# A fused decoder kernel on one core: the same items of work in another written-out order

## The reference

```
x = ln(x + L0_attn(x))     # 16 heads, xpos rotation, causal
x = ln(x + L0_xattn(x, ctx))
x = ln(x + L0_ffn(x))      # quantised linear, depthwise conv, silu, quantised linear
x = ln(x + L1_attn(x))     # attention over the 16 heads inside each token
x = ln(x + L1_xattn(x, ctx, mask))
x = ln(x + L1_ffn(x))      # 16 experts, top 2, capacity
x = ln(x + L2_attn(x))     # 16 heads, rotation, causal
x = ln(x + L2_xattn(ctx, x, ctx, mask))
x = ln(x + L2_ffn(x))      # gated, then two 512x512 layers
x = ln(x + L3_attn(x))     # one head, distance bias
x = ln(x + L3_xattn(x, ctx, ctx))
x = ln(x + L3_ffn(x))      # 8 experts, gated
```

## Time and profile before

| | |
|---|---|
| median of three runs | 1619.02 us |
| the profiled execution | 1613.98 us |
| its span in the trace | 1612.3 us |
| TensorE busy | 1322.0 us, 8762 matmuls |
| VectorE busy | 1094.0 us |
| ScalarE busy | 742.5 us |
| GpSimd busy | 363.0 us |
| granted TensorE clock, mean | 0.913 of 2.4 GHz |

### The profile page before, as it was taken

One profiled execution on the slowest core, in us unless ns is written; L12 is line 12 of the kernel. 1 busy time (PEld: TensorE's weight loads), 2 busy tenths in 40 slices (PEclk: granted clock), 3 DMA queues, 4 the chain that ended last, 5 costly groups with the idle time before them and its releaser, 6 DMA issues.

```text
span 1612.3 us, 24326 instructions
## 1 busy us (share of the span) xinstructions
PE 1322.0 (82%) x8762; PEld 612.3 (38%) x8762; DVE 1094.0 (68%) x2373; ACT 742.5 (46%) x1040; POOL 363.0 (23%) x470
## 2 busy tenths in 40 slices
PE   4586997876557688687789997999999999978986
PEld 2233332332222343343235544434444444434453
DVE  4674777889999778988877675763335522358665
ACT  1046565654424324214367642565745543534742
POOL 2224253105243404333631120121311100110000
PEclk8688899997767789899799999999999999999989
DMA  6521043200020210321232223130313220033111
GB/s 157 149 61 45 19 93 62 42 2 1 1 39 16 54 41 25 79 64 31 52 79 49 69 60 77 60 84 19 88 25 55 66 81 28 1 76 67 32 46 44
DMA packets 50354, 86.26 MB, mean 53 GB/s; under 512 B 13750, under 2 KB 42230, under 8 KB 45942
## 3 DMA queue, kind: packets, MB, share of 16 engines
q1 hardware_dynamic: 50238, 84.71, 22.5%
HBM read 66.95 MB, written 15.60 MB: 51 GB/s over the span
## 4 chain that ended last, share of the span: by engine, by line
PE 50%; DVE 26%; issue 6%; DMA 5%; ACT 5%; SPq 4%; POOL 3%; ACTq 0%; DVEq 0%; POOLq 0%
PE ps L910 6%; PE ps L1064 6%; PE ps L836 6%; DVE MX L1279 6%; PE ps L1030 4%; PE ps L1037 4%; PE ps L1031 4%; PE ps L843 3%; DMA KH<-scratch 2%; PE ps L871 2%; PE ps L792 2%; DVE pack L1420 2%; DVE HEADS L1431 2%; SPq L2055 2%; DVE HEADS L1422 2%
## 5 line engine op out<-in xcount | busy, mean ns | idle before, releaser
L1279 DVE TENSOR_REDUCE MX<-ps 128x3 f32<-128x462 f32 (+5 forms) x704 | 412.0, 627 | 136.5 <-PE ps L843 113.1
L1710 ACT ACTIVATE WORK<-ps 128x1024 f32<-128x1024 f32 (+1 forms) x352 | 318.9, 945 | 143.7 <-PE ps L871 112.5
L836 PE MATMUL ps<-KH,QH 48*128 48x154 bf16 (+5 forms) x1536 | 139.1, 267 | 107.4 <-DVE MX L1279 61.6
L910 PE MATMUL ps<-WORK,VA 128*18 128x512 f32 (+3 forms) x1536 | 163.8, 514 | 9.8 <-POOL WORK L1951 9.0
L1804 ACT ACTIVATE SIDE<-ps 128x512 f32<-128x512 f32 x96 | 56.9, 597 | 234.8 <-PE ps L1031 234.7
L1951 POOL TENSOR_SCALAR_AFFINE_SELECT WORK<-WORK 128x256 f32<-128x256 f32 (+1 forms) x192 | 93.3, 494 | 297.1 <-ACT WORK L1710 296.7
L1965 POOL TENSOR_TENSOR HEADS<-HEADS 128x512 f32<-128x512 f32 x64 | 106.0, 1690 | 239.5 <-DVE HEADS L1432 132.1
L836 PEld LDWEIGHTS ps<-KH,QH 48*128 48x128 bf16 (+1 forms) x1536 | 60.3, 96 | 262.1 <-DVE MX L1279 150.0
L1037 PE MATMUL ps<-SIDE 128*128 128x128 f32 x768 | 111.6, 295 | 23.2 <-DVE SIDE L1530 20.0
L1530 DVE TENSOR_TENSOR SIDE<-SIDE,ps 128x512 f32<-128x512 f32 x96 | 65.5, 686 | 91.0 <-ACT SIDE L1804 90.7
L871 PE MATMUL ps<-QH,KH 54*128 54x512 bf16 (+3 forms) x768 | 116.7, 345 | 10.7 <-ACT WORK L1710 7.0
(11 more groups left out here) (285 smaller groups left out, 2149.8 us busy)
## 6 DMA issues: line engine op xcount, KB each, us to landing
SIDE<-in_experts SPq DMA_DIRECT2D x96, 192.0 KB, 2.4
scratch<-HQ SPq DMA_DIRECT2D x48, 192.0 KB, 2.9
QH<-scratch SPq DMA_DIRECT2D x48, 192.0 KB
SIDE<-in_wide SPq DMA_DIRECT2D x8, 1024.0 KB, 6.0
QH<-scratch SPq DMA_DIRECT2D x48, 128.0 KB
scratch<-HK SPq DMA_DIRECT2D x16, 192.0 KB, 3.0
QH<-scratch SPq DMA_DIRECT2D x48, 64.0 KB
KH<-scratch SPq DMA_DIRECT2D x16, 192.0 KB
```

Of the source, the lines that this page charges most:

```text
L836: mms[b] = pe.matmul(banks[b][:, c * pitch:c * pitch + width], qr[b][:, h, t * 128:t * 128 + 128], kr[b][:, h, 0:width], start=(c == 0), s ...
L910: mm = pe.matmul(ps[32 * j:32 * j + 2 * NV, UB, q0:S], lhsT.rearrange("p a c -> p (a c)"), PB[:, (PAIR_BASE[F] + where[pi]) % NSLOT, b, at ...
L1279: dve.tensor_reduce(MX[:, 32 * b + i0:32 * b + i0 + cnt], src, AX.X, ALU.max, negate=True).then_inc(freed, 1)
L1710: act.activation(PB[:, N % NSLOT, :, lo:hi], wide_banks("pair", F, n)[:, :, lo:hi], ACT.Exp).then_inc(sem("exp_done"), 1)
```

## The change

Only the text `STEPS` changes. It has the same words in the same numbers (1986 words, 2338 items with each `max` counted as two), and `FRONT_ORDER`, `SIDE_ORDER` and `TAIL_ORDER` are as before, so each kind still passes through its stages, batches and numbers in the same sequence; what moves is how the kinds are interleaved. The waits are the same by their rule, with counts that follow the new list. The functions that do the work are not touched. Below is the start of both texts and the lines in which the prediction's steps can be found.

```diff
@@ -255,76 +255,79 @@
 STEPS = """
-project*5 pieces send base project*5 max*2 pieces max*2 project max project max*5 project max*2 project max*2 send max
-project max*4 pieces max*3 split project max turn max project max pair*2 max*2 pair max pair*2 max value max pair value
-max value max project max pair*2 max pair max send value max pair*2 max value pair max value max pair value pair max
-value copy pair max pair max value max pair*2 max pair split pair out value pair max pair turn value max pair value max
-pair value max value pair max value pair max pair value max copy pair*2 max value max project pair max value max pair
-out pair max pair*2 max value mix pair project value*2 pieces value rest pair max value pair max pair max value pair max
-pair*2 max send wo max copy value max value square pair max pair*2 max mean value split value x max pair project*2 turn
...
-value*2 pair max pair copy wo max value send max square pair mean max value x max pair split project value pair*2 turn
...
-project mix pair max value pair max pair project split wo copy pieces out value send turn max value max square pair mean
...
-log ew x qkv top ew gu project*2 ew rank gu project dn ew project pieces hv dn gu hs dn ew hm send hv gu*2 qkv dn ew dn
...
-project out max pair*2 max project*2 mix max pair*2 max value max pair pieces max pair*2 max value max wo copy send pair
-max square value max value max split mean value x copy turn out*2 project*3 mix project pair*2 max wo pair*2 max square
...
-hid2 wo x square hid2 mean x wo project*2 f3 square mean turn s3 project s3 project pair fk3 pieces pt3*2 value pt3*2 x
...
+project*5 pieces base send max*2 project max*2 project max*2 project max project max project max pieces max project
+max project max*2 project max*3 project max*2 rest send max*2 project max pieces max split project max turn pair max
+pair max project pair max pair*3 max value pair max*2 pair value max send pair*2 value max value pair max value max*2
+pair value max pair max value*2 pair copy max pair max value pair max project max*2 pair*2 value max pair project
+value max pair max pair split max pair value pair max turn max out pair max value pair value*2 pair*2 max value pair
+max pair*2 copy max project max*2 value*2 max pieces out pair max*2 pair max pair value mix max pair*2 value max pair
+value*2 max pair wo pair*2 max value pair max value pair max square copy value max pair value pair*2 max mean send max
...
+pair out max pair value pair x pair max value split value max value project value project value turn max pair project
...
+pair*2 mix value out value send wo turn square max pair*2 max pair value copy max mean out max x mix max*2 wo square
...
+ew project*2 hs rank pieces send dn gu hv ew max gu ew max dn max hm qkv ew gu max dn gu ew max dn max gu max ew dn
...
+project value max out value max copy square out max mean max mix max split wo project pieces x send turn square max
...
+square hid2 mean x wo project*2 f3 turn pair square s3 project s3 project fk3 pair value pt3*3 pieces pt3 pair mean
...
 """.split()
```

More of the change, by code:

```diff
@@ L273 @@
[L273 to L282, removed]
@@ new lines @@
+pair*2 max value max mean pair x project max value pair*2 q0x value pair*2 project max q0t project max split h0*2 copy
+silu0 value project out value silu0 pieces turn value silu0*2 send copy h0t*2 pair out h0b pair h0b h0t mix wo h0t
+pair h0b square max mean max h0b x pair*2 max wo max*2 q0x pair max value pair value*2 copy pair q0t pair max out max
+h0*2 value square max pair value mean value silu0 max*2 split silu0 x silu0*2 copy h0t turn h0t pair h0b pair h0t pair
+h0b qkv h0t pair h0b pair out qkv mix value hs hv value wo value pair copy pair square hs pair mean qkv hm pair x hv
@@ new lines @@
+h0b hs out pair qkv wo hm q0x square value q0t hs hv value hm value h0 copy hv out h0 silu0*3 mix hm silu0 mean wo h0t
+square ht x mean wo square h0t mean x h0b*2 x h0t qkv project*2 h0t h0b qkv project h0b hs project pieces send wo hv
+q0x square hs max*2 q0t max hm qkv hv max h0 max h0 max*2 silu0 qkv silu0 max silu0 max silu0 max*2 split h0t*2 turn
+h0b pair*2 hs pair h0t value pair hm mean pair h0b value h0t h0b pair h0b pair value copy hv hs hm wo pair*2 value x
+pair value*2 out copy hv square out hm mix mean wo x ht qkv wo square*2 mean x mean x log ew project*2 qkv top gu hs
@@ new lines @@
+dn max*2 project max hm project ew*2 max gu*2 project max ew dn max qkv max ew project max dn max ew gu pieces max gu
+max dn max gu max send dn max split ew gu dn hv max ew gu dn turn dn max pair acc max pair wo square max pair*2 max
+mean pair max pair x qkv project*3 hs project*2 pieces value*2 pair hm pair value pair max pair*3 hv max value*2 send
+pair value pair hs pair*2 max*2 value pair max value copy split hm pair value turn pair*2 value pair value pair max
+pair out pair max value hv max value max value*2 max value hm copy pair*3 value max pair out value max pair ht pair
@@ new lines @@
+gu copy dn ew*2 out*2 gu dn max split gu ew dn max ew gu dn max gu dn ew max gu dn max ew*2 gu dn max ew gu dn max ew
+gu turn max dn gu ew dn max gu mix pair max wo max dn square max value dn max pair*2 acc max pair wo square mean pair
+max mean max x*2 pair wide pair max value project max pair project max pair project w3 project max g2*2 value max g2
+max g2 project max pieces send hid2 split turn copy hid2 max value pair max pair hid2 max value pair max pair value
+max pair out copy max pair*2 value max pair*2 value pair max pair value max pair value pair max pair value*2 wide max
@@ new lines @@
+pair out value max pair mix pair value max copy wo max pair*2 value*2 pair max out pair value max square pair*2 value
+max pair mean max pair hid2 max value*4 max copy hid2 out max hid2 max split x hid2 mix turn hid2 wo pair*2 square wo
+pair*2 mean pair value wide x pair value pair project pair g2 project*2 g2 project g2 pieces square send g2 pair mean
+hid2*3 pair max value max pair value pair*2 max pair value*2 max value pair value copy max pair value pair max pair*2
+out pair max value x pair*2 wide max value*2 max pair*2 hid2 max value*4 copy max hid2 split out hid2 mix hid2 wo
@@ new lines @@
+hid2 out hid2 mix hid2 max pair wo pair max square hid2 max pair value max wo max pair mean max pair value x pair max
+value wide pair max copy square g2*2 value max g2*2 wide pair value max pair hid2 split hid2*3 turn value mean copy
+out hid2*2 out hid2 x mix hid2 wo pair*2 wo f3 square mean square s3*2 fk3 value pt3*2 pair pt3*2 mean pair x pair x
+wo f3 square pair mean s3 x s3 value pair value pt3*2 fk3 pt3*2 copy project*2 wo log pair project ew top square pair
+project value ew*2 pair value mean gu*2 x pieces value out copy send dn*2 gu max project max dn ew max ew gu max
```

74 lines of the change are left out of this document (31 added, 43 removed).

## The result

The changed kernel takes 1647.57 us (median; 1639.21 to 1650.70) against 1619.17 us for the kernel before: a ratio of 1.0169, 95% interval 1.0129 to 1.0209. The profiled execution took 1646.09 us, its span is 1644.4 us and its mean granted clock 0.902 (before: 1613.98, 1612.3 and 0.913).

The account below looks back on a forecast made before the run. TensorE was taken to bound the kernel (work plus 290 us of idle), VectorE being fuller from 250 to 800 us. Terms -12 + 4 + 34 - 3 - 4 = +19 us gave 1638 us; own case 1625 to 1652, range 1602 to 1668.

Parts of the forecast that it names:

- parts 3 and 4: Waits from short cover behind `turn` and `send`: 30.9 us outside 250 to 800 us, 29.3 inside; taken +34 us.
- Part 1: `rest` comes 154 places earlier, into L0a.0's maxima where ScalarE idles, so TensorE's 11.97 us wait goes; taken -12 us.
- Part 2: L0a.1's projections move from the free wait for L0a.0's keys to among the first maxima; taken +4 us.
- Part 3: `turn` to first `pair`: work between falls short of 3.8 us; missing cover over all fronts grows from 6.4 to 34.7 us.
- Part 3's and 4's weighting by stretch: Waits outside 250 to 800 us counted whole, inside half since VectorE is fuller there: 45.6 us, times 0.75.
- Part 4: Operands and weights behind `send` get less cover: missing 14.1 us more outside 250 to 800 us, 17.8 inside.
- Parts 5 and 6: ScalarE's table reloads fall from 80 to 72, taken -3 us; TensorE's waits ahead of the experts' `dn` shrink, taken -4.
- A: Rival: faster, short cover hides as VectorE sets the pace and waits fall on existing idle; -15 us, 1604 us; chance 0.18.
- B: Rival: much slower, all 60 us show as a waiting TensorE starves VectorE of its three banks; 1664 us; chance 0.22.
- C: Rival: no change in time, local gains and losses cancel; 1619 us; chance 0.07.
- D: Rival: `rest` stalls as long in its new place, its ScalarE work held up by late weights; 1650 us; chance 0.06.

Follow-up runs that it names:

- the two kernels with one edit each: Kernel before with only `rest` moved early: 1623.43 us, ratio 1.0015; kernel before with only L0a.1's and L0a.2's projections moved late: 1616.90 us, ratio 0.9978.
- operands late: Kernel before with projections, pieces and send of L0x.2, L1x.1, L1x.3, L2x.1 and L3x.0 moved down: 1666.22 us, ratio 1.0276.
- both early edits: Kernel before with `rest` moved early and L0a.1's and L0a.2's projections put among L0a.0's maxima: 1611.98 us, ratio 0.9957.
- three bare turns: Kernel before with the first pair directly behind `turn` for L0a.3, L0x.1 and L0x.3: 1635.93 us, ratio 1.0078.
- middle alone: Kernel before with only items 245 to 697 in the new order: 1652.04 us, ratio 1.0194.
- eight bare turns: Kernel before with the first pair of eight fronts pulled up behind `turn` or the last pair of the front before: 1654.15 us, ratio 1.0207.
- turns covered: Changed kernel with each front's first pairs held behind `turn` until about 4 us of other work, then let go together: 1665.22 us, ratio 1.0267 to before.
- covered evenly: Changed kernel with each front's pairs and what follows delayed behind `turn` by a queue, let go one by one: 1687.44 us, ratio 1.0401 to before.
- tail alone: Kernel before with only items 698 to the end in the new order: 1616.48 us, ratio 0.9989.

## Why the prediction was right

- **Sign, range and the sum of idle.** The sum was +19 us of idle; the page has +17.5. That agreement is luck, as the places show: the forecast had two thirds of the idle of parts 3 and 4 outside 250 to 800 us, and at equal work TensorE's idle grows by 16.5 us between the cuts, falls by 1.5 us behind them (168.4 to 166.9) and grows by about 2.5 us ahead of them. Too little was charged in the middle, and in the tail the gains were put too low. The median stands 10 us above the forecast and the sum had no term for the clock, which is worth 14.6 us of busy time in the pair of profiles.
- **The missing term.** "The order can change idle time only" is the sentence that failed. The earlier trace rows showed a clock between 0.82 and 0.99 by stretch, so it was there to be read that TensorE's busy time is not a constant.
- **Part 1, -12.** The wait for ScalarE is gone in the changed kernel, and it has VectorE wait 0.63 us for the biases where it was 20.11. ScalarE's last instruction of `rest`, TensorE's first, VectorE's copy:

```profile
77.80 0.63 ACT L1669 ACTIVATE pack<-HEADS 128x256 f32<-128x256 f32 x1
...
80.42 0.83 PE L772 MATMUL ps<-pack,HEADS 128*128 128x2 f32 x6
...
85.37 0.17 DVE L1206 COPY BROWS<-ps 128x6 f32<-128x6 f32 x1 [0.63 <-PE ps L777]
```

  The forecast had TensorE there "near 80" and ScalarE done at 74; they are 80.42 and 78.4. But the 12 us depend on part 2, as the two kernels with one edit each show, and in the changed kernel they are not a gain: up to the first cut it takes 181.9 us against 181.5, with a scatter of 5 us. L0a.0's keys are waited for 8.3 us longer and its first pair 3.3 us.
- **Part 2, +4.** Wrong in sign: together with L0a.2's projections it gives 0.22%, 3.6 us. The step that failed priced the projections in their new place only: TensorE's first wait for keys grows by 6.3 us, but that is the time in which it did this work before. In their new place they cost nothing that can be seen; why the sum is even a little below nothing was not separated.
- **Part 3.** The mechanism is as described. L0a.0 and L2x.2 of the changed kernel, `turn` and first `pair`:

```profile
97.13 0.40 PE L856 MATMUL ps<-const,MP 128*48 128x128 bf16 x4 [0.68 <-DVE WORK L1265]
101.43 0.61 PE L874 MATMUL ps<-QH,KH 54*128 54x512 bf16 x2 [3.90 <-DMA QH<-MT]
...
1237.81 0.40 PE L856 MATMUL ps<-const,MP 128*48 128x128 bf16 x4
1242.08 0.41 PE L887 MATMUL ps<-QH,KH 54*32 54x512 bf16 x8 [3.87 <-DMA QH<-MT]
```

  The forecast named 3.8 us as what must be covered (its own rows give 4.33 - 0.59 = 3.7) and "near 3.8" for L2x.2; it is 3.87. Of 34.7 us missing cover, 27.3 show (0.79; taken 0.75). What was mis-sized is the price of one: about 1.1 us of time for each us of wait between the cuts, 1.4 to 1.7 behind them.
- **Part 3's and 4's weighting by stretch.** Inside 250 to 800 us a wait was counted half, "since VectorE is fuller there". The order of the two was right and both weights were too low. Bare turns added to before's order cost about 1.1 times their wait between 181 and 427 us, where VectorE is 85% busy (12.8 us of waits cost 14.2 in one run, 4.0 cost 4.4 in another), and 1.4 to 1.7 times behind it. In the changed kernel the loss still lies all in the first of these stretches, for two other reasons: there the rest of the new order adds its 18 us, and behind it the new order takes away waits (10.5 us at `dn`, 9.8 at `project`), of which the sum had 4.
- **Part 4.** The waits for keys were to grow most at L1x.1 and L1x.3, and this failed. The changed kernel has no wait for keys at either; what TensorE waits at their first maxima, 1.5 and 0.6 us, ends with VectorE. Waits for keys (before, then after) grow at L0a.0, from 16.1 to 24.5 us, and at L1x.0, the one line with MK; L3x.2's 8.3 us shrink to 1.4.

```profile
PE ps L836 <- DMA KH<-scratch: 28.0, 5, 16.1
PE ps L836 <- DMA KH<-MK: 3.2, 1, 3.2
...
PE ps L839 <- DMA KH<-MK: 9.6, 1, 9.6
```

  Why L1x.0 waits longer, with about the same work between its keys and its maxima, stays open. The weights behind a `send` did grow, 13.1 to 20.9 us, as in the run with operands late, where the queue's next load pays and not the front's own maxima.
- **Parts 5 and 6.** 73 table loads as forecast (36 + 19 + 10 + 4 + 4 in the trace), and ScalarE is busy for 11.2 us less; its effect on the time was not measured by itself. The gain at `dn` is 10.5 us of waits, 4 taken. "From 800 to 1400 us TensorE's idle grows by 10 us or more" came true, 29.4 to 43.6 us, but these windows hold different work; at equal work the tail's idle does not grow.

- **The rivals.** A (faster, waits fall on idle that exists) describes the tail and not the middle. B (all of it shows, since VectorE's banks run empty) describes the middle, where VectorE is idle for 33 us longer; over the whole kernel its wait for L846 grows by 64.5 us. C is excluded by the interval, and D did not come about.

## What to carry to other kernels

Price a wait of TensorE at its length, and where TensorE is full at half as much again or more: what comes behind it ran at the lower clock for some us, so sum idle and busy time separately and expect both to move. Such a price tells the worth of a wait, not of a whole order, which may give it back elsewhere, as the tail did. Compare two orders at cuts where both have done the same items; windows between such cuts say in which stretch a loss arises, and a list spliced at the cuts shows whether it does so by itself. Moving the one item that waits seldom helps in an order this tight: look at which queue it stands in and at what stands behind it there, since on ScalarE and on SyncE the neighbour pays.

## What the runs showed of the hardware that was not expected

More waits mostly go with a lower clock: span and clock of the profiled executions are 1609.3 us at 0.913 (both early edits), 1612.3 at 0.913 (before), 1634.4 at 0.904 (three bare turns), 1644.4 at 0.902 (after), 1650.3 at 0.899 (middle alone), 1652.1 at 0.895 (eight bare turns), 1663.0 at 0.888 (turns covered) and 1688.8 at 0.881 (covered evenly). The run with the tail alone does not fit, 1615.7 us at 0.901, with 1333.4 us of busy time and 8 us less idle than before. And the clock differs between executions of one kernel: 23 of before took 1612.15 to 1628.12 us, the fastest at 0.914 and the slowest at 0.900.

In one wait of 4.78 us it fell to its lower level, in the middle of a stretch where it is 0.99 otherwise, and the same matmul form then took 2.07 instead of 1.02 us, twice as long, as the two levels stand to each other. In both runs that have this wait the fall came inside it, and the clock rose again while TensorE worked.
